# Masking the diagonal window after the transpose instead of before it, in the attention of a recurrent layer and its gate

## What is computed

```
q, k, v = split(xn @ w_qkv)           # 16 heads of 128
q, k = xpos(q), xpos(k)               # rotation by tables of cos and sin
s = (q k^T / sqrt(128)) * decay_mask  # causal: 0 above the diagonal
y = group_norm(s v);  s = (silu(xn @ w_g) * y) @ w_proj
g = silu(router(xn) picks: xn + bias | xn + low rank | transformer_layer(xn))
out = x + s * g
```

## Time and profile before

| | us |
|---|---|
| median of 2 runs | 7801.91 |
| lowest and highest of them | 7746.45, 7857.36 |
| the profiled execution, device time | 7639.17 |
| its span on the slowest core | 7637.6 |
| spans of the eight cores | 7577.1 to 7637.6 |

### The profile page before, as it was taken

The page is one execution under the profiler, slowest core; times in us unless marked ns, Lnnn a source line. Parts: engine busy times, 40 slices in busy tenths (PEclk is TensorE's granted clock), DMA queues, the critical chain, the costliest instruction groups (busy, mean ns, idle before and its releaser), DMA issues.

```text
span 7637.6 us, 64883 instructions; the slowest of 8 cores (7577.1 to 7637.6 us)
## 1 busy us (share of the span) xinstructions
PE 4083.3 (53%) x18468; PEld 1840.6 (24%) x18468; DVE 1650.1 (22%) x3916; ACT 2633.5 (34%) x3196; POOL 362.5 (5%) x314
## 2 busy tenths in 40 slices
PE   1456565555555853345444454444536488656465
PEld 1222222222222310122212222122212133222122
DVE  5522222222222125311111111111110300011111
ACT  4122323233333456244444444444431144311011
POOL 0000000000000100000000000000000011111010
PEclk9977676767666965666666676666766699978687
DMA  3122121222220740001000010001113377799897
GB/s 96 39 33 36 21 34 23 32 25 29 26 29 12 90 51 0 0 10 20 10 10 10 10 20 10 10 10 13 11 35 39 50 87 89 102 108 99 140 96 105
DMA packets 762994, 319.23 MB, mean 42 GB/s; under 512 B 702096, under 2 KB 726800, under 8 KB 757552
## 3 DMA queue, kind: packets, MB, share of 16 engines
q0 software_dynamic: 703296, 201.61, 27.5%
q1 hardware_dynamic: 59376, 113.48, 4.6%
HBM read 474.69 MB, written 41.94 MB: 68 GB/s over the span
## 4 chain that ended last, share of the span: by engine, by line
PE 40%; ACT 20%; DVE 14%; issue 13%; DMA 12%; DVEq 1%; ACTq 0%; SPq 0%; POOLq 0%; POOL 0%
DMA wff<-ff2T 5%; ACT L946 4%; PE pbB L775 4%; PE pbA L775 4%; DMA wqh<-ff1T 3%; PE pbB L1690 3%; PE pbB L716 3%; PE pbA L716 3%; ACT scp L946 3%; ACT L930 2%; PE pbA L657 2%; DVE scT_sb L1004 2%; PE pbA L1552 2%; ACT L784 2%; PE pbS L1017 2%
## 5 line engine op out<-in xcount | busy, mean ns | idle before, releaser
L946 ACT ACT_TABLE_LOAD x320 | 410.6, 1283 | 459.7 <-DVE ybuf L1029 278.2
L784 ACT ACT_TABLE_LOAD x128 | 164.2, 1283 | 891.6 <-PE pbA L775 483.8
L1017 PE MATMUL pbY<-vtok,scT_sb 128*128 128x128 bf16 x1024 | 129.5, 306 | 555.7 <-DVE scT_sb L1004 555.7
L1017 PE MATMUL pbS<-vtok,scT_sb 128*128 128x128 bf16 x1280 | 143.0, 288 | 462.8 <-DVE scT_sb L1004 462.8
L1690 PE MATMUL pbA<-xn_allT,wff 128*128 128x512 bf16 x1024 | 257.8, 419 | 195.0 <-DMA wff<-ff2T 151.8
L930 ACT ACT_TABLE_LOAD x192 | 246.3, 1283 | 318.9 <-PE pbA L921 317.7
L1552 PE MATMUL pbA<-bufA,wqh 128*128 128x512 bf16 x1024 | 246.5, 397 | 174.5 <-DMA wqh<-ff1T 92.7
L775 PE MATMUL pbB<-xn_allT,wvh 128*128 128x512 bf16 x1024 | 305.7, 466 | 51.1 <-DVE vtok L801 38.2
L1690 PE MATMUL pbB<-xn_allT,wff 128*128 128x512 bf16 x1024 | 255.5, 416 | 139.1 <-DMA wff<-ff2T 139.1
L1743 ACT ACT_TABLE_LOAD x32 | 41.1, 1283 | 785.7 <-DVE cb_g L1733 785.7
L1561 ACT ACT_TABLE_LOAD x128 | 164.2, 1283 | 407.6 <-PE pbA L1552 306.5
(11 more groups left out here) (298 smaller groups left out, 6767.8 us busy)
## 6 DMA issues: line engine op xcount, KB each, us to landing
wff<-ff2T POOLq DMA_DIRECT2D x32, 2048.0 KB, 24.6
wqh<-ff1T POOLq DMA_DIRECT2D x64, 512.0 KB, 9.1
p0x<-x_all SPq DMA_DIRECT2D x16, 1024.0 KB, 5.8
xn_allT<-hg_sp SPq DMA_DIRECT2D x2, 8192.0 KB, 35.5
p0x<-x_own SPq DMA_DIRECT2D x8, 1024.0 KB, 5.8
wqh<-w_qkv POOLq DMA_DIRECT2D x16, 512.0 KB, 8.1
wkh<-w_qkv POOLq DMA_DIRECT2D x16, 512.0 KB, 7.1
wvh<-w_qkv POOLq DMA_DIRECT2D x16, 512.0 KB, 7.6
```

Of the source, the lines that this page charges most:

```text
L784: self.inc(s.activation(vt[:, 0:cw], pb[key][:, 0:cw], AF.Identity), s_s)
L946: self.inc(s.activation(scp[:, e0:e0 + ew], pb[key][:, e0 - c0:e0 - c0 + ew], AF.Exp, bias=self.biasT[:, rt:rt + 1], accum_out=self.den_sb ...
L1017: inst = t.matmul(pb[ykey][:, 0:P], self.scT_sb[:, st * P:(st + 1) * P], self.vtok[:, st * P:(st + 1) * P], start=(st == 0), stop=(st == n ...
```

## The change

The transposes now take all their blocks from the unmasked `scp`. The mask is applied by DVE as it takes the window's two transposed blocks out of PSUM: a multiplication by `ltriT_sb`, the mask transposed, takes the place of that part of the copy. So a group's copy that contained the window is split in a copy of the blocks ahead of it (if the group has any) and a multiplication of 256 columns. In "ret" the window multiplication of `stage_scores` is gone. In "ffn" it stays, since the denominator is summed from it, but the transposes don't read its result or wait for it. The new mask is loaded by one more DMA, the second of the constants.

```diff
         def _(s):
             self.dma(s, "consts", ltri_sb[:], ltri_d[:])
+            self.dma(s, "consts", ltriT_sb[:], ltriT_d[:])
             self.dma(s, "consts", eye_sb[:], eye_d[:])
...
-                def _(v, rt=rt, W=W, scp=scp):
-                    self.wt(v, *st_scb[rt], *self.g_wtp[rt % 2])
-                    self.inc(v.tensor_tensor(self.wt_pair[rt % 2][:],
-                                             scp[:, W - 256:W],
-                                             self.ltri_sb[:], op=ALU.mult), s_v)
-                self.V(_)
-                st_win[rt] = self.tok(s_v)
+                if kind == "ffn":
+                    def _(v, rt=rt, W=W, scp=scp):
+                        self.wt(v, *st_scb[rt], *self.g_wtp[rt % 2])
+                        self.inc(v.tensor_tensor(self.wt_pair[rt % 2][:],
+                                                 scp[:, W - 256:W],
+                                                 self.ltri_sb[:], op=ALU.mult), s_v)
+                    self.V(_)
+                    st_win[rt] = self.tok(s_v)
...
-                        self.wt(t, *st_scb[rt], st_win[rt], *self.bfree[tkey])
+                        self.wt(t, *st_scb[rt], *self.bfree[tkey])
                         for k in range(nk):
                             st = g0 + k
-                            if st >= nst - 2:
-                                src_ = self.wt_pair[rt % 2][:, (st - (nst - 2)) * P:
-                                                            (st - (nst - 2) + 1) * P]
-                            else:
-                                src_ = scp[:, st * P:(st + 1) * P]
                             inst = t.transpose(pb[tkey][:, k * P:(k + 1) * P],
-                                               src_, self.eye_sb[:])
+                                               scp[:, st * P:(st + 1) * P],
+                                               self.eye_sb[:])
...
-                        self.inc(v.tensor_copy(self.scT_sb[:, g0 * P:(g0 + nk) * P],
-                                               pb[tkey][:, 0:nk * P]), s_v)
+                        nw = max(0, (g0 + nk) - (nst - 2))
+                        nc_ = nk - nw
+                        if nc_ > 0:
+                            iv = v.tensor_copy(self.scT_sb[:, g0 * P:(g0 + nc_) * P],
+                                               pb[tkey][:, 0:nc_ * P])
+                        if nw > 0:
+                            iv = v.tensor_tensor(
+                                self.scT_sb[:, (nst - 2) * P:nst * P],
+                                pb[tkey][:, nc_ * P:nk * P],
+                                self.ltriT_sb[:, 0:nw * P], op=ALU.mult)
+                        self.inc(iv, s_v)
```

More of the change, by code:

```diff
@@ L67, in host_consts @@
     ltri = keep.astype(BFDT)
+    jl = np.arange(P)[:, None]
+    ii = np.arange(P)[None, :]
+    ltriT = np.concatenate([(2 * ii + half >= jl).astype(BFDT),
+                            (2 * ii + half >= jl + 128).astype(BFDT)], axis=1)
     eye = np.eye(P, dtype=BFDT)
@@ L72, in host_consts @@
         pmatT[2 * q, 2 * q + 1] = 1.0
-    return ltri, eye, pmatT.astype(BFDT)
+    return ltri, ltriT, eye, pmatT.astype(BFDT)
 def cvec(v, cfg):
@@ L164, in build @@
         ltri_d = dbf("ltri", [P, 256])
+        ltriT_d = dbf("ltriT", [P, 256])
         eye_d = dbf("eye", [P, P])
@@ L205, in build @@
         ltri_sb = self.sbuf("ltri_sb", [P, 256], BF16)
+        ltriT_sb = self.sbuf("ltriT_sb", [P, 256], BF16)
+        self.ltriT_sb = ltriT_sb
         ones_col = self.sbuf("ones_col", [P, 1], BF16)
@@ L1000, in stage_consume, with _ @@
                     tg = self.tok(s_t)
-                    def _(v, g0=g0, nk=nk, tkey=tkey, tg=tg):
+                    def _(v, g0=g0, nk=nk, tkey=tkey, tg=tg, nst=nst):
                         self.wt(v, tg, *self.g_scT, *self.g_yb2)
-                        self.inc(v.tensor_copy(self.scT_sb[:, g0 * P:(g0 + nk) * P],
-                                               pb[tkey][:, 0:nk * P]), s_v)
+                        nw = max(0, (g0 + nk) - (nst - 2))
[9 more added lines that the diff above has]
+                        self.inc(iv, s_v)
                     self.V(_)
@@ L1845, in host_inputs @@
     cq, sq, ck, sk = xpos_tables(cfg, half)
-    ltri, eye, pmatT = host_consts(cfg, half)
-    m.update(cq=cq, sq=sq, ck=ck, sk=sk, ltri=ltri, eye=eye, pmatT=pmatT)
+    ltri, ltriT, eye, pmatT = host_consts(cfg, half)
+    m.update(cq=cq, sq=sq, ck=ck, sk=sk, ltri=ltri, ltriT=ltriT, eye=eye,
+             pmatT=pmatT)
     return m
```

## The result

| | us, or ratio |
|---|---|
| changed kernel, median of 11 runs | 7604.84 (7437.35 to 7694.4) |
| kernel before, median of 10 runs | 7742.9 (7627.44 to 7918.67) |
| ratio, after to before | 0.9727, 95% interval 0.9625 to 0.9829 |
| profiled execution after, slowest core (before) | 7578.3 (7637.6) |

The change makes the kernel faster by 2.7%, with an interval of 1.7 to 3.8%. The forecast was 1.7%, at the near edge of it; its time of 7667 us and its range hold.

A forecast was written before the change was run, and what follows sets the result against it. VectorE's copies in "ret" were held behind the next round's window multiplication. -141 ("ret") +7 ("ffn") +2 (start) = -132 us on 7639, scaled to the 7802 median: 7667 us, range 7500 to 7740.

The forecast's parts named there:

- What bounds the kernel: In "ret", VectorE's copies stand behind the next round's window multiplication, which idles 2.68 us for ScalarE in the fourth round.
- the bound from above: Most that "ret" could gain: VectorE's 113 waits of L959 for ScalarE's L930, 206.7 us.
- The gain in "ret": Copies start when their transposes are done: 8.79 us a head, 141 us over 16 heads.
- handover of 0.24 us: Gap assumed in "ret" from the end of the transposes to the start of VectorE's copy, called a cautious value.
- the transposes' dropped wait: Transposes no longer wait for the window multiplication; said to give nothing in "ffn", and given no gain in "ret".
- rival 3: Denser "ret" rounds 3 to 6 get the higher clock: 70 us more saved, 7596 us; chance 0.12.
- The price of the split: Copy plus multiplication from bf16 PSUM, taken at 0.29 us, costs 0.07 us more than the single copy.
- rival 1: Multiplication from PSUM costs 0.42 us, in "ret" and "ffn": -101 us in sum, 7699 us; chance 0.24.
- What is late next: In "ret", ScalarE: round 4 shrinks from 7.3 to 4.9 us, its two evictions take 3.8, so it just keeps up.
- Rival 2: ScalarE's evictions slip behind and "ret" transposes wait, losing half the gain there: -62 us, 7739 us; chance 0.12.
- "Ffn": Nothing gained in the "ffn" attention; splitting copies adds 0.07 us in 6 rounds of 16 heads, 7 us.
- The start: One more DMA in the chain of constants delays the first tile of x, counted as 2 us.

The follow-up runs named there:

- e3: Changed kernel with the window multiplication of "ret" put back in its old queue place, its result unread; ratio to the kernel before 1.0029, "ret" heads 124.8 us.
- e4: Kernel before, with the "ret" window multiplication of the next round moved behind the copy of ybuf in VectorE's queue; ratio 0.9806, "ret" heads 115.5 us.
- e8: The changed kernel as it is, run and profiled again; ratio to the kernel before 0.9737.
- e9: The change in "ret" alone, "ffn" in its old form, second run of that kernel; ratio to the kernel before 0.955.
- e1: The change in "ret" alone, "ffn" in its old form, first run; median 7510.53 us against 7668.13 of the kernel before, no ratio.
- e10: The change in "ret" alone, with old-form "ffn" whose window and sums move behind the copy of ybuf; ratio to the kernel before 0.9165.

## Why the prediction was right, point by point

**What bounds the kernel.** Right, and shown by e3 and e4: one waiting instruction of the next round, and its place in VectorE's queue. One reading of the prediction was loose. The 113 waits of L959 for L930 are those of rounds 0 to 5 and 7 and one of round 6. The 16 of round 0 (29.4 us) hold no copy back, and in round 6 it was TensorE that the window waited for. So the bound from above was 177 us and not 206.7; 161 were won.

**The gain in "ret".** Right in mechanism and round by round, and too small: 8.79 us a head forecast, 10.1 measured. The start-to-start times of the products on core 0, in us, as a mean over the 16 heads (worked out from the timelines of TensorE), against what the prediction's rounds amount to. The first row is the way from the second round's scores to the first products:

| products of rounds | before | after (e8) | gained | forecast |
|---|---|---|---|---|
| scores to 0 | 3.72 | 1.70 | 2.02 | 1.95 |
| 0 to 1 | 4.27 | 3.61 | 0.66 | 0.65 |
| 1 to 2 | 4.42 | 3.36 | 1.06 | 0.97 |
| 2 to 3 | 6.52 | 4.09 | 2.43 | 2.21 |
| 3 to 4 | 7.05 | 4.43 | 2.62 | 2.38 |
| 4 to 5 | 7.43 | 6.76 | 0.67 | 0.35 |
| 5 to 6 | 7.74 | 7.26 | 0.48 | 0.35 |
| 6 to 7 | 4.56 | 4.68 | -0.12 | -0.07 |

The rows add up to 9.8 us, and over all eight cores to 45.76 - 35.70 = 10.1. The term that was mis-sized is small in each round. First, the handover of 0.24 us was too cautious: 514.04 to 514.14 is 0.10, and 524.63 to 524.81 is 0.18. Over the heads of core 0 in e8 the mean is 0.14. Second, I priced the transposes' dropped wait at nothing, and in round 0 it is something: the window had only just been multiplied. The transposes started 0.72 us behind the scores (518.02 to 518.74) and now start 0.38 behind (513.24 to 513.62). In the first head the way to the first products shrank by 2.37 us, from 3.82 to 1.45. In most others it was 3.69 before and is 1.69, so that the mean is near the forecast by some luck.

Third, some rounds run at the higher clock, which is rival 3 in small. Ten products took 0.82 us in the head above, which at the lower level is 1.23. The clock and the time of a round go together. Here is the interval from the products of round 3 to those of round 4 in two heads of e8, core 0, as in the earlier trace rows (the clock is the third number from the end):

```profile
758.82:763.00 4.18, 2.66 (x21) 1.56 (x22) 1.87 (x4) 4.02 (x6) 0.00 (x0) 0.75 0.02 4
871.89:876.53 4.64, 3.36 (x21) 2.21 (x22) 1.87 (x4) 3.90 (x5) 0.00 (x0) 0.50 0.00 0
```

In ten heads this interval takes 4.57 to 4.64 us, at a granted clock of 0.50 to 0.60, and in six 3.83 to 4.29, at 0.74 to 1.00. Before, it took 7.01 to 7.05 us in all 16, also in the three in which the clock was 0.72 to 0.74. So at the lower level the gain was 2.4 us, which is the forecast's 2.38, and the rest of the 2.62 is the clock. Between rounds 4 and 5 it is 0.5 us at the lower level (7.43 to 6.94), against 0.35, and 0.2 more from the clock. The mean of the products fell from 305 and 285 ns to 299 and 274 in the "ret" stage of core 0, and its granted clock rose from 0.70 to 0.73.

**The price of the split.** Right: 282 ns, where 0.29 was taken and 0.42 was rival 1. The Trainium skill's rate for tensor_tensor with a PSUM operand ("VectorE: DVE Perf Modes", section "The perf-mode tier table (the rule you actually need)") does not hold for a bf16 bank here: 256 columns take no longer than the 292 ns from SBUF. The measurement decides.

**What is late next.** Round 4 shrank to 4.4 us in the mean, not 4.9, with two evictions of 1.9 in it, and still the transposes did not wait for ScalarE (0.8 us in all). Rival 2 did not come.

**"Ffn".** The split was forecast at 7 us, 0.42 a head. The heads grew by 0.8 us, 12 us in all. Of that 0.5 also show in e9, where "ffn" is in its old form, so the split itself costs about 0.3 us, 5 us in all. By the rounds it is 0.39: the seven product times of a head add up to 67.98 us in e9 and 68.37 in e8 (core 0). Where the 0.5 us come from is open, as the rounds of e9 are no longer than the 68.13 of the kernel before.

**The start.** 2 us forecast; the first load of x is issued 2.0 us later (10.10 to 12.07 in the mean).

**The sum.** -132 us forecast. By the stages -161 + 12 + 2 make -147. The middle's 16 us, which I had no step for, bring it to -163, and the end is 5 us longer. The mean span of the eight cores fell by 160 us, from 7612.9 to 7453.0 (e8), which is 2.1%, inside the interval; the middle is 0.2 of it. That the time of 7667 us comes close is in part luck. It is the profiled execution scaled up to the median of two runs, 7801.91 us, and the median of ten was 7742.9. On the scale of the profiled execution 7507 us stand against the 7481.36 of e8, and the three shortest runs of the changed kernel, 7437.35 to 7476.6 us, lie below the range.

**The chances.** I put 0.61 on a change within 2% and 0.35 on more than 2% faster. It was more, by the point of the ratio; its interval reaches to both sides of 2%, so the runs don't decide between the two.

## What to carry to other kernels

Ask of an engine that works in program order what stands between a finished input and the instruction that needs it. One waiting instruction of the *next* round in that place cost 10 us a head here, though nobody needed it soon, and moving it behind that round's copies brought 9 of them without the new mask. Then look for the same pattern elsewhere before polishing the first: in the softmax attention it was worth 25 us a head, more than twice as much.

## What the runs showed of the hardware that I had not expected

- VectorE multiplies 256 columns of a bf16 PSUM bank by a bf16 SBUF tile in 282 ns (256 times, on the page of the changed kernel). The forecast had taken 0.29 without a row for it. From f32 banks 512 columns took 687 ns, and the eviction of 256 took 425.
- TensorE's granted clock in one and the same round differs from head to head. Between the products of rounds 3 and 4 it was 0.74 to 1.00 in six heads of e8 (core 0) and 0.50 to 0.60 in ten. With it the round took 3.83 to 4.29 us in place of 4.6.
- The time of the same loads in the same place of the program differs between kernels that differ elsewhere. ff2T, 2 MB at a time, landed in 20.6 to 21.5 us (median of a core) in the three profiles e1, e9 and e10, and in 23.7 to 25.7 us in all others. That is 100 us of the whole, more than half of what this change brought. The cause is open.
